# Attention by pairs of heads: stacks, maximum banks, denominators and the value run rearranged

## The reference

```python
query = seq2 + b_self
key   = concat([x + b_prev, seq2 + b_self])
value = concat([x, seq2])
q, k, v = query @ Wq + bq, key @ Wk + bk, value @ Wv + bv      # 16 heads of 32
score_prev = q . k[:l1] * SCALE, masked to keys < seq_len1      # 512 x 512 for each head
score_self = sum(q * k[l1:]) * SCALE                            # one score for each row: itself
weights = softmax(concat([score_prev, score_self]))
attn = weights[:-1] @ v[:l1] + weights[-1] * v[l1:]
x = x + attn @ Wo + bo
h = gelu(x @ W1 + b1)                                           # 2048 hidden
x = x + concat([h @ W2 + b2, h @ We[indices] + be[indices]])
```

## Time and profile before

| what | value |
|---|---|
| median of the 3 runs | 1779.17 us (1777.35 to 1780.21) |
| span of the profiled execution | 1777.1 us, from first to last instruction |
| what lies around the span | not in the profile; the median is 2.07 us above it |
| busy TensorE matmul / weight loads | 1711.9 us / 1257.8 us |
| busy VectorE / ScalarE / POOL | 913.1 / 707.3 / 646.7 us |
| granted TensorE clock, mean | 0.983 |
| chain that ended last | TensorE 82%, DMA 5%, VectorE 5%, SP's queue 4% |

### The profile page before, as it was taken

The page is one execution under the profiler, slowest core; times in us unless marked ns, Lnnn a source line. Parts: engine busy times, 40 slices in busy tenths (PEclk is TensorE's granted clock), DMA queues, the critical chain, the costliest instruction groups (busy, mean ns, idle before and its releaser), DMA issues.

```text
span 1777.1 us, 27938 instructions
## 1 busy us (share of the span) xinstructions
PE 1711.9 (96%) x8256; PEld 1257.8 (71%) x8256; DVE 913.1 (51%) x1434; ACT 707.3 (40%) x1255; POOL 646.7 (36%) x517
## 2 busy tenths in 40 slices
PE   5999999999999999999997999999999999999998
PEld 5766656666666666666662788888888888888886
DVE  4567576775866757758578643232232323232322
ACT  3254354443544545435454443323242323233321
POOL 3167576574874937758565301000010101010000
PEclk8999999999999999999996999999999999999999
DMA  6452545433534435244334433223241413232211
GB/s 138 84 106 65 108 86 116 83 95 74 122 87 96 98 85 118 66 109 85 87 102 136 127 104 54 76 46 80 47 89 41 89 53 65 71 53 72 47 30 24
DMA packets 369116, 147.34 MB, mean 83 GB/s; under 512 B 289098, under 2 KB 329034, under 8 KB 369042
## 3 DMA queue, kind: packets, MB, share of 16 engines
q1 hardware_dynamic: 359590, 143.65, 35.7%
q10 hardware_dynamic: 9452, 2.88, 0.7%
HBM read 69.36 MB, written 26.23 MB: 54 GB/s over the span
## 4 chain that ended last, share of the span: by engine, by line
PE 82%; DMA 5%; DVE 5%; SPq 4%; issue 3%; ACT 1%; POOL 1%; DVEq 0%; ACTq 0%; POOLq 0%
PE ps_proj L1313 14%; PE ps_max L1344 7%; PE ps_av L1265 6%; PE ps_av L1267 6%; PE ps_av L1266 6%; PE ps_av L1384 6%; PE ps_score L1371 5%; DMA stacks<-parts 4%; PE ps_proj L1265 3%; PE ps_max L1267 3%; PE ps_max L1266 3%; PE ps_max L1265 3%; PE ps_proj L1266 3%; PE ps_proj L1267 3%; PE ps_score L1265 3%
## 5 line engine op out<-in xcount | busy, mean ns | idle before, releaser
L747 ACT ACTIVATE p_f<-ps_score 128x512 f32<-128x512 f32 x512 | 303.9, 599 | 441.7 <-PE ps_score L1371 407.2
L969 DVE TENSOR_REDUCE m_col<-ps_max 128x1 f32<-128x512 f32 x512 | 329.0, 684 | 213.6 <-PE ps_max L1344 212.1
L622 POOL TENSOR_TENSOR p_sum<-p_sum,p_f 128x512 f32<-128x512 f32 x256 | 323.5, 1297 | 3.3 <-ACT p_f L747 3.3
L1165 DVE TENSOR_TENSOR h_lo<-h_f,h_hi 128x512 fp32r<-128x512 f32 x128 | 88.0, 688 | 405.9 <-ACT h_hi L851 405.6
L662 POOL TENSOR_TENSOR z_f<-z_f,a_raw 128x512 f32<-128x512 f32 x28 | 35.8, 1289 | 663.5 <-ACT z_f L860 639.2
L619 POOL TENSOR_TENSOR p_sum<-p_f 128x512 f32<-128x512 f32 x128 | 161.5, 1292 | 201.3 <-PE ps_av L1393 195.8
L1344 PE MATMUL ps_max<-stacks 97*128 97x512 f32 x512 | 188.5, 435 | 28.9 <-DMA stacks<-parts 14.3
L1313 PE MATMUL ps_proj<-in_hi,w_hi 128*128 128x512 f32 x512 | 205.5, 401 | 10.6 <-POOL in_lo L627 7.3
L1371 PE MATMUL ps_score<-stacks 99*128 99x512 f32 x512 | 208.4, 418 | 5.7 <-ACT p_f L747 5.5
L1313 PE MATMUL ps_proj<-in_lo,w_hi 128*128 128x512 f32 x512 | 204.2, 399 | 0.0
L1313 PE MATMUL ps_proj<-in_hi,w_lo 128*128 128x512 f32 x512 | 203.8, 398 | 0.0
(11 more groups left out here) (131 smaller groups left out, 2700.1 us busy)
## 6 DMA issues: line engine op xcount, KB each, us to landing
stacks<-parts SPq DMA_DIRECT2D x384, 128.0 KB
raw<-in_x_dram SPq DMA_DIRECT2D x128, 64.0 KB, 2.2
raw<-in_fside_BxSxS_dram SPq DMA_DIRECT2D x128, 64.0 KB, 2.2
den<-own_scratch SPq DMA_DIRECT2D x128, 64.0 KB, 2.8
attn_scratch<-num SPq DMA_DIRECT2D x32, 256.0 KB, 3.0
x_raw<-in_x_dram SPq DMA_DIRECT2D x128, 64.0 KB, 2.1
we_raw<-in_L_cond_We_dram SPq DMA_DIRECT2D x32, 256.0 KB, 2.9
a_raw<-attn_scratch SPq DMA_DIRECT2D x31, 256.0 KB, 3.4
```

Source lines behind the costliest of these rows:

```text
L622: pool.tensor_tensor(p_sum[:, j], p_sum[:, j], now, ALU.add).then_inc(sum_made, 1)
L747: act.activation(p_f[:, i % FLIGHT], ps_score[i % 2][:, :], ACT.Exp, scale=SCALE).then_inc(p_made, 1)
L969: dve.tensor_reduce(m_col[:, n % C, n // C:n // C + 1], ps_max[n % 2][:, :], AX.X, ALU.max).then_inc(max_made, 1)
```

## The change

- Score tiles come by pairs of heads: tiles 0 to 7 are heads 0 and 1, tiles 8 to 15 heads 2 and 3, each over its four key blocks (`tile_at`, `place_of`). p_f has one place for each tile. POOL's sums follow the same order.
- The stacks go out as two pairs: pair 0 before the maxima rows, pair 1 after them and after the spread of the denominators. The mask row goes once for a pair, with semaphores of its own.
- ps_max has three banks, ps_av becomes the one bank ps_num. The 16 maximum tiles stand at steps 0 to 10. Own scores, turned maxima and denominators use the first 128 columns of the maximum banks and stand at step 11.
- Denominators: 16 matmuls of 128x8 weights by 128 columns into one 128x128 tile (row 32t + j for head j, query block t). VectorE adds own_s, takes one reciprocal of 128x128 in SBUF, and four SBUF to SBUF transfers spread it over all rows (`over_den`). Own weights are spread in the same way, without DRAM.
- All 16 value matmuls of a group stand in one run after its tile 15.
- VectorE: at step 12 the den sum of G-1, the normalization of G-2 (both inputs in SBUF), then the maxima rows; at step 13 the reciprocal and the numerator of G-1; at step 14 qk_f. The store is of G-2.
- Values of a batch by thirds over steps 0 to 5; in_hi 4 to 7 all at (1, 15); POOL's in_low in two batches of four; transposes moved.

The core of the diff:

```diff
+def tile_at(i):
+    n, rest = divmod(i, PAIR)
+    return rest // 2, 2 * n + rest % 2
+def place_of(t, j):
+    return PAIR * (j // 2) + 2 * t + j % 2
 def sums_of(G, t, j):
-    return SUMS * G + HG * (t - 1) + j + 1
+    return SUMS * G + 2 * (C - 1) * (j // 2) + 2 * (t - 1) + j % 2 + 1
+def added(n):
+    half, rest = divmod(n, 2 * (C - 1))
+    return 1 + rest // 2, 2 * half + rest % 2
 def stack_count(b, c):
-    return DMA * (3 * (2 * b + c // 2 + 1) + b + 1)
+    return DMA * 3 * (2 * b + c // 2 + 1)
 def tiles_of_max(i):
-    ends = (2, 4, 6, 8, 10, 12, 14, TILES)
+    ends = (2, 4, 5, 7, 8, 10, 11, 13, 14, 15, TILES)
     return range(ends[i - 1] if i else 0, ends[i]) if i < len(ends) else range(0)
-turn_at = {(1, 3): (0,), (1, 4): (1,), (1, 7): (2,), (1, 8): (3,), (1, 11): (4,), (1, 12): (5,),
-           (1, 15): (6,), (2, 0): (7,)}
-in_hi_at = {(1, 5): (0,), (1, 6): (1,), (1, 8): (2,), (1, 9): (3,), (1, 15): (4,), (2, 0): (5,), (2, 1): (6,), (2, 2): (7,)}
-in_lo_at = in_hi_at
+turn_at = {(0, 9): (0,), (0, 11): (1,), (0, 13): (2,), (0, 14): (3,), (1, 9): (4,), (1, 13): (5,),
+           (1, 14): (6,), (1, 15): (7,)}
+in_hi_at = {(1, 5): (0,), (1, 6): (1,), (1, 7): (2,), (1, 9): (3,), (1, 15): (4, 5, 6, 7)}
...
-k_at, q_at = (6, 4, 4, 4), (8, 7, 8, 7)
+def thirds_of(g, i, first):
+    plain = (0, 1, 2, 4, 5, 7, 8, 9, 11, 12, 13, 14)
+    slots = ((6, 6, 7, 7, 8, 9, 10, 11, 12, 12, 13, 14), plain, (0, 1, 2, 5, 6, 7, 8, 9, 11, 12, 13, 14), plain)[g]
+    return [n for n, at in enumerate(plain if first else slots) if at == i]
+def value_thirds_of(i):
+    return [n for n, at in enumerate((0, 0, 1, 1, 2, 2, 3, 3, 4, 4, 5, 5)) if at == i]
+v_out_at = {2: 0, 3: 1, 5: 2, 6: 3}
+def k_at(g, first):
+    return 8 if g == 0 and not first else 4
+def q_at(g, first):
+    return 10 if g == 0 and not first else 8
 def first_max(t):
...
                          blocks(src, b, j % C, q)).then_inc(in_landed[j % 4], DMA)
-    def stack(b, c, j):
+    def stack_pair(b, c, n):
         G, r = C * b + c, c % 2
-        if j == 0:
+        if n == 0:
             wait(sp, q_lo_made, G + 1)
             wait(sp, k_lo_made, G + 1)
-        wait(sp, score_mm, TILES * (G - 2) + HG * (C - 1) + j + 1)
         if c < 2:
-            sp.dma_start(f(k_st[KM - 1:KM, r, j]), mask_dram[bass.ds(b, 1)]).then_inc(stacked[r][j], DMA)
-        rows = slice(DH * j, DH * (j + 1))
-        for n, pair in enumerate((parts[rows, 1:3], parts[rows, 0:3:2], parts[rows, 1:4:2])):
-            sp.dma_start(f(stacks[DH * n:DH * (n + 1), r, j]), f(pair)).then_inc(stacked[r][j], DMA)
+            wait(sp, score_mm, TILES * (G - 2) + place_of(C - 1, 2 * n + 1) + 1)
+            sp.dma_start(f(k_st[KM - 1:KM, r, 2 * n:2 * n + 2]), mask_dram[bass.ds(b, 1)]).then_inc(masked[r][n], DMA)
+        for j in (2 * n, 2 * n + 1):
+            wait(sp, score_mm, TILES * (G - 2) + place_of(C - 1, j) + 1)
+            rows = slice(DH * j, DH * (j + 1))
+            for part, pair in enumerate((parts[rows, 1:3], parts[rows, 0:3:2], parts[rows, 1:4:2])):
+                sp.dma_start(f(stacks[DH * part:DH * (part + 1), r, j]), f(pair)).then_inc(stacked[r][j], DMA)
     def maxima(b, c, tiles):
...
     def own_weights(b, c):
-        G, r = C * b + c, c % 2
-        sp.wait_ge(ow_stored, DMA * (G + 1))
-        wait(sp, attn_made, G - 1)
-        for j in range(HG):
-            sp.dma_start(den[DH * j:DH * (j + 1), r].rearrange("d (t q) -> d t q", q=P),
-                         own_dram[r, :, j].partition_broadcast(DH)).then_inc(ow_landed[r], DMA)
+        G = C * b + c
+        sp.wait_ge(ow_made, G + 1)
+        for t in range(C):
+            sp.dma_start(own_rows[:, P * t:P * (t + 1)], rows_of(own_s[c % 2], t)).then_inc(ow_landed, DMA)
+    def over_den(b, c):
+        G = C * b + c
+        sp.wait_ge(rden_made, G + 1)
+        for t in range(C):
+            sp.dma_start(over_den_rows[:, P * t:P * (t + 1)], rows_of(den, t)).then_inc(over_den_landed, DMA)
     def store(b, c):
...
+            if last and g == 3:
+                wide_late(EARLY)
+                wide_late(EARLY + 1)
+                wide_late(EARLY + 2)
+                attended(0, 3)
+                residual(0, 1)
+                residual(0, 2)
+                residual(0, 3)
+            if not (first and g == 0):
+                over_den(*after(b, g, -1))
             if more:
-                for j in range(HG):
-                    stack(*after(b, g, 2), j)
+                stack_pair(*after(b, g, 2), 1)
             if last and g == 2:
                 for n in range(9, EARLY):
                     wide(n)
...
                 attended(0, 1)
                 residual(0, 0)
                 attended_apart()
-            if not (last and g == C - 1):
+            if bound:
                 own_weights(*after(b, g, 1))
-            if last and g == 3:
-                wide_late(EARLY)
-                wide_late(EARLY + 1)
-                wide_late(EARLY + 2)
...
+            if not (first and g == 0):
+                for n in range(SUMS // 2, SUMS):
+                    add_probabilities(*after(b, g, -1), n)
+            if g == 1 and not last:
+                for j in range(C):
+                    in_low(b + 1, j)
+            own_value(b, g)
+            for n in range(SUMS // 2):
+                if n == 4 and g == 1 and not last:
+                    for j in range(C, 2 * C):
                         in_low(b + 1, j)
-                if i == 8:
-                    own_value(b, g)
-                n = (i + 7) % TILES
-                if i >= 9:
-                    add_probabilities(b, g, 1 + n // HG, n % HG)
-                elif n < SUMS and not (first and g == 0):
-                    add_probabilities(*after(b, g, -1), 1 + n // HG, n % HG)
+                add_probabilities(b, g, n)
...
         act.wait_ge(own_mm, G + 1)
-        wait(act, ow_stored, DMA * G)
-        act.copy(own_s[:, :], ps_max[1][:, 0:P]).then_inc(own_made, 1)
+        wait(act, ow_landed, HG * DMA * (G - 1))
+        wait(act, den_made, G - 1)
+        act.copy(own_s[c % 2][:, :], ps_own).then_inc(own_made, 1)
...
-        T = TILES * (C * b + g) + i
-        act.wait_ge(score_mm, T + 1)
-        wait(act, av_mm, T - FLIGHT + 1)
-        t, j = i // HG, i % HG
-        wait(act, sum_made, sums_of(C * b + g - 1, max(t, 1), j))
-        act.activation(p_f[:, i % FLIGHT], ps_score[i % 2][:, :], ACT.Exp, scale=SCALE).then_inc(p_made, 1)
+        G, (t, j) = C * b + g, tile_at(i)
+        act.wait_ge(score_mm, TILES * G + i + 1)
+        wait(act, av_mm, C * (G - 1) + t + 1)
+        wait(act, sum_made, sums_of(G - 1, max(t, 1), j))
+        act.activation(p_f[:, i], ps_score[i % 2][:, :], ACT.Exp, scale=SCALE).then_inc(p_made, 1)
...
         G = C * b + g
-        dve.wait_ge(ov_made, G + 1)
-        dve.wait_ge(den_mm, HG * (G + 1))
-        dve.tensor_tensor(den[:, g % 2], ps[:, :], den[:, g % 2], ALU.add).then_inc(den_made, 1)
+        dve.wait_ge(ow_made, G + 1)
+        dve.wait_ge(den_mm, G + 1)
+        wait(dve, over_den_landed, HG * DMA * G)
+        dve.tensor_tensor(den[:, :], ps, own_s[g % 2][:, :], ALU.add).then_inc(den_made, 1)
+    def one_over_den(b, g):
...
+        G = C * b + g
+        dve.wait_ge(den_made, G + 1)
+        wait(dve, attn_made, G)
+        dve.reciprocal(den[:, :], den[:, :]).then_inc(rden_made, 1)
     def wide_low(n):
         hi, lo = wide_parts(n)
...
-    def normalize(b, g, in_bank=True):
-        G, r = C * b + g, g % 2
-        dve.wait_ge(rden_made, 4 * (G + 1))
+        dve.wait_ge(over_den_landed, HG * DMA * (G + 1))
         dve.wait_ge(num_made, G + 1)
-        over_den = ps_den[:, :] if in_bank else den[:, r]
-        dve.tensor_tensor(num[:, r], num[:, r], over_den, ALU.mult).then_inc(attn_made, 1)
+        dve.tensor_tensor(num[:, r], num[:, r], over_den_rows, ALU.mult).then_inc(attn_made, 1)
     def bias_sums(w):
...
                         turn(b + 1, j)
-                if i == k_at[g] + 1 and project:
+                if i == k_at(g, first) + 1 and project:
                     k_low(*nxt2)
-                if i == q_at[g] + 1 and project:
+                if i == q_at(g, first) + 1 and project:
                     q_low(*nxt2)
-                if i == 9 and bound:
+                if i == 12 and started:
+                    denominator(*after(b, g, -1))
+                    if not (first and g < 2):
+                        normalize(*after(b, g, -2))
+                if i == 12 and bound:
                     own_max(*nxt)
                     m_parts(*nxt)
                     own_less_max(*nxt)
-                if i in (13, 14) and started and not (last and g == C - 1):
-                    for n in range(2) if i == 13 else range(2, 4):
-                        one_over_den(*after(b, g, -1), n)
-                if i == 13 and project:
+                if i == 13 and started:
+                    one_over_den(*after(b, g, -1))
```

(50 more changed lines are left out.)

229 lines of the change are left out of this document (117 added, 112 removed).

## The result

| | before | after |
|---|---|---|
| median of the runs, us | 1779.69 (4 runs) | 2032.17 (2025.96 to 2037.58, 4 runs) |
| ratio, 95% interval | | 1.142 [1.1394, 1.1446] |
| profiled execution: span, us | 1777.1 | 2024.1 |
| first score tile of batch 0 to that of (batch 7, group 2), us | 854 | 1049 |
| from there to the end, us | 848 | 902 |

The account below looks back on a forecast made before the run. TensorE, busy 96% of the span, was taken as the bound. Of 62 us of stalls, less 17.6, 12, 3 and 1.7, 28 go; plus 4.5 at the end, 32: 1745 profiled, 1747 median; own range 1737 to 1758, wider 1724 to 1776.

Parts of the forecast that it names:

- the paragraph on the stacks: SP's queue: stacks leave sooner by pairs, the wait at a group's start goes; four added spread transfers cost 2.5 us.
- own weights without the DRAM hop: Own weights spread directly from SBUF: POOL waited for them off the path, so the effect is nothing.
- Rival D: SP full in groups 0 and 1: stacks in time, loads and transposes late; about 1779, as before; chance 0.05.
- Stalls: TensorE's section of 854.3 us, put at 792.7 without stalls, so 62 us of stalls, 2.0 a group.
- small steps that stay: Small stalls in the section's groups assumed to remain: 0.4 us a group, 12 us in all.
- Normalize: VectorE step 12: collides with POOL's sum in every group, lasts 1.6 us, delays the value run; 17.6 us lost.
- Rival A: Normalize on VectorE costs nothing, so the 17.6 us are saved too: 1730; chance 0.25.
- B: Rival: normalize starves behind POOL's sums; 1858 if every one lasts 5.14 us; slower than before, chance 0.11.
- Clock: About 3 us of the section's 62 come from a lower granted clock, 0.99, and were left in.
- The end: Last two groups: half a value run less and VectorE spared about 3 us of reciprocals, -4.5 us together.
- Narrow denominators: TensorE: 16 matmuls of N=128 for four of N=512 take 0.88 us against 0.86, so nothing.
- C: Rival: narrow denominators pay for weight loads, 0.7 us a group, +21, 1768; chance 0.14 with other new waits that size.

Follow-up runs that it names:

- rows32: Changed kernel, its eight spreads reading 32 neighbouring SBUF partitions 4 times each instead of 4 partitions 32 times (other values, for timing only): 1748.5 us.
- normalize_late: both_by_dram with last denominators wide and last-group store order as before the change, normalize at step 15 (last group 12), store ahead of spread: 1733.4 us.
- both_by_dram: Changed kernel with own weights and one over the denominator spread through DRAM, the latter last in SP's group: 1755.8 us.

## Why the prediction was wrong

**The step that failed** is a price in the paragraph on the stacks: "on SP four spread transfers are added, 2.5 us at the stacks' price", and with it "22.7 of some 25 us: full, not over", and own weights without the DRAM hop at "nothing". A stack reads 32 partitions once; a spread reads four neighbouring ones 32 times over, a form of which the trace before has no row, and I took the nearest row for its price and set no upper bound on it. Its price is 5.9 to 6.5 us of issuing and 11.7 us from issue to landing. SP's issues from one pair of maxima rows on are 1.4 + 5.9 + 8.0 + 6.2 + 2.2 + 11.0 + 4.0 (the next six stacks), 38.6 us; in rows32 the same seven rows are 23.0, where I had 22.7. The same price stood behind pair 1 of the stacks "by 1.5 us into the next group". The wait at a group's start did go, but pair 1 was issued only by 9.8 us, and TensorE waited 81 us for it in 21 places, at the ninth maximum tile. Rival D named half of the mechanism (SP full, loads and transposes late), held the stacks to be in time, and priced it as if SP's load were known, at 1779 with 0.05; the true price is after less rows32, 284 us.

Everything else was tried by rows32, which is the change with a spread at the assumed price: 1748.5 us against the forecast 1747. That closeness is partly luck, as the terms show:

- *Stalls.* The section without any was put at 792.7, 794.4 with the value run that moves in. normalize_late's is 806.6, so 12.2 remain, the size of the 12 for "small steps that stay"; what they consist of was not looked into.
- *Normalize.* It lasts 1.56 us in the median of both_by_dram, forecast 1.6. But its cost was put at 17.6 us, and taking it away brought the section from 814.3 to 806.6, 7.7. With X for the start of score tile 12 again, the numerator of group 1 is done at X+4.1 in both_by_dram, where I had X+4.3 and a transpose more: normalize lasts only 0.85 us in group 1, so the collision does not come "in every group". The run could start at X+3.9, not X+3.8, and waits about 0.4 us in groups 2 and 3, 0.3 in group 1 and 0.1 in group 0. Rival A (nothing) and the forecast each had half. B did not come: the longest in both_by_dram is 1.68 us.
- *Clock.* 3 us were left in for it; the granted clock of the section is 1.00 once TensorE no longer stalls for long. With normalize this makes the section 12 us better than forecast, 814 against 826.
- *The end.* Forecast -4.5, in rows32 +10 (857.9 from (7,2) on, against 848.0), in both_by_dram +20. I counted matmuls and reciprocals there and followed neither the store that now comes a group later nor the last spread, which nothing covers. This undid the 12, and that is the luck in 1748.5.
- *Narrow denominators.* From the first of their sixteen matmuls to the own scores behind them it is 0.88 us in both_by_dram (660.19 to 661.07), as forecast: C is out. That the blocks' two changes of mode cost nothing more and that the reduce is late for no tile stands: groups of 36.1, 24.3, 24.9 and 24.4 us where 35.5, 25.5, 24.9 and 24.9 were forecast.

My sign for D, "groups at 25.5 and more with SP never idle", is what the profile showed, though D's own price was far off.

## What to carry over

A transfer that repeats a few rows is priced by where those rows lie, not by its bytes: look for a row of the same form, and where there is none, bound it from above by all its bytes passing one after another. Such a price counts twice, as time of the queue and as lateness of what is issued behind it, so the second thing to write down is how much slack the next transfer has: here 11.7 us ahead of pair 1 cost 81 us of waits and 7.5 us ahead of it 5. And a change that postpones work by a step of the pipeline has to be followed through the last steps, where nothing runs beside it.
